# Half of the loads of x issued from ScalarE's DMA queue, the rest and the weights from SyncE's

## Chip, cores and metric

The kernel runs on one core of a Trainium2 chip. Its time is the device time of one execution in microseconds (us); less is better. One execution was also profiled: the profile gives each instruction's start and length on the engines PE (TensorE matmul), PEld (TensorE weight load), DVE (VectorE), ACT (ScalarE), POOL (GpSimd) and SP (SyncE), and what each of them waited for. SPq is the queue of SyncE's DMA issues.

## The reference

One layer of decayed linear attention with a gate, then a feed-forward part with routed low-rank adapters, each followed by a residual and a layer norm. x has 4 x 256 tokens of 512 features; there are 32 heads of 128.

```python
qkv = silu(x @ qkv_w.T)                       # 32 heads, q, k, v of 128
# per head, in blocks of 32 tokens:
scores = einsum(q, k) * diag_decay
out = scores @ v + (q * q_decay) @ kv
kv = kv * block_decay + (k * k_decay).T @ v
normed = norm_w * attn * rsqrt(mean(attn * attn) + eps)
x = layernorm(x + (sigmoid(x @ gate_w.T) * normed) @ out_w.T)
base = x @ base_W.T + base_b
w = softmax(x @ router_W.T + router_b)        # mapped to 8 experts
x = layernorm(x + base + 2 * ((x @ A.T) * w) @ B)
```

## The kernel before

Every product is made of float32 numbers split into a high and a low part (`xh`, `xl` for x; `wh`, `wl` or, for the first weights, `yh`, `yl`), with three matmuls for one: high by high, high by low, low by high. ACT makes the high parts, DVE the low ones. The heads go in 8 groups of 4. Weights come as blocks from `stream` through the two slots of `stage`; a block may only be loaded when the one two before it has been split (semaphore `t_lo`). All orders are written out by hand, one program for each engine, with semaphores between them, and all DMAs of this kernel stand in SyncE's program.

Only the start matters here. x arrives as eight pieces of 128 x 512 (`x_load(0)` to `x_load(7)`, from `xt` into `acc`, which is called `quad` in the code, 256 KB each), each with a semaphore of its own, `x_in[i]`. The first weight block arrives in three pieces: 128 KB (`w_first`), 128 KB (`w_in[0]`) and 256 KB (`w_in[1]`). ACT's `first_group` (from L738) takes them in a fixed order: first weights, x 0, second weights, x 1, third weights, x 2, then x 3 to x 7; before that it loads its activation table and runs a small warming SiLU (L1057). PE has seven matmuls on zeros (L2354) to begin with. Then `first_pieces(0)` to `first_pieces(7)` (L2190, L2196, L2199) do six matmuls for each piece of x: two of high by high, two with the weights' low part, two with x's low part. Piece 1 needs x 1 and the second weights, piece 2 needs x 2 and the third weights, pieces 3 to 7 only their x. The values of the first group (L2007 to L2009) and then all other work follow in PE's order.

After the loads of x, SyncE issues the second block of weights (L396, L397), two decay tables (L404), six small constants (L429) and the third block, which waits on `t_lo`.

Of the kernel before, what the change touches and what calls it, by code (L numbers as in the profile page):

```python
# [82 lines left out]
def load_no(g, name):  # L83

    if g == 0:
        return LOADS0.index(name)
    return len(LOADS0) + (g - 1) * len(LOADS) + LOADS.index(name)
# [22 lines left out]
def splits_of_load(m):  # L110

    if len(LOADS0) <= m < TAIL_LOAD and LOADS[(m - len(LOADS0)) % len(LOADS)] in ("va", "oa"):
        return 2 * m + 3
    return 2 * m + 2
# [36 lines left out]
def build(nc, stream, xt, x, decay, norm_w, base_b, lora_router, router_b, expert_map, ident_in, ones_in, fresh_in, out):  # L151
    ctx = ExitStack()
    with ctx:
# [3 lines left out]
        def sem(name):  # L157
            return ctx.enter_context(nc.semaphore(name))
# [81 lines left out]
        quad = acc[:, :, :].rearrange("p t n -> p (t n)").rearrange("p (q n) -> p q n", q=4)  # L240
# [9 lines left out]
        x_in = [sem(f"x_in{i}") for i in range(8)]  # L250
# [45 lines left out]
        def half(i):  # L296
            return slice(i * W, i * W + W)

        def tile(t):
            return slice(t * P, t * P + P)  # L300
# [80 lines left out]
        @block.sync  # L381
        def _(sp):
            def block_load(m):

                s = m % 2
                if m >= 2:
                    sp.wait_ge(t_lo, splits_of_load(m - 2))
                sp.dma_start(stage[:, s, 0, :], stream[m, :, 0, :]).then_inc(t_in[s], 16)
                sp.dma_start(stage[:, s, 3:8:2, :], stream[m, :, 1:4, :]).then_inc(t_in[s], 16)

            def rows_load(m, n=2):

                s = m % 2
                if m >= 2:
                    sp.wait_ge(t_lo, splits_of_load(m - 2))
                sp.dma_start(stage[:, s, 0:n, :], stream[m, :, 0:n, :]).then_inc(t_in[s], 16)  # L396
                sp.dma_start(stage[:, s, n:2 * n, :], stream[m, :, n:2 * n, :]).then_inc(t_in[s], 16)  # L397

            def load_decay(h):
                if h >= HEADS:  # L400
                    return
                if h >= 2:
                    sp.wait_ge(s_full, 2 * (h - 2) + 2)
                sp.dma_start(dec[:, h % 2, :], decay[h]).then_inc(dec_in[h % 2], 16)  # L404

            def next_group(g, name):
                if g + 1 < GROUPS:
                    block_load(load_no(g + 1, name))
                else:
                    rows_load(TAIL_LOAD + ["qk0", "va", "vb"].index(name))  # L410

            def x_load(i):
                sp.dma_start(quad[:, i // 2, half(i % 2)], xt[i // 2, :, half(i % 2)]).then_inc(x_in[i], 16)

            sp.dma_start(stage[:, 0, 0:2, tile(0)], stream[0, :, 0:2, tile(0)]).then_inc(w_first, 16)
            x_load(0)
            sp.dma_start(stage[:, 0, 0:2, tile(1)], stream[0, :, 0:2, tile(1)]).then_inc(w_in[0], 16)
            x_load(1)
            sp.dma_start(stage[:, 0, 2:4, :], stream[0, :, 2:4, :]).then_inc(w_in[1], 16)
            for i in range(2, 8):  # L420
                x_load(i)
            rows_load(1)
            load_decay(0)
            load_decay(1)
            for dst, src in ((nw[:, :], norm_w), (ident[:, :], ident_in), (ones[:, :], ones_in),
                             (rb[:, :], router_b.partition_broadcast(P)),
                             (emap[:, :], expert_map.partition_broadcast(P)),
                             (fresh[:, :], fresh_in.partition_broadcast(P))):
                sp.dma_start(dst, src).then_inc(const_in, 16)  # L429
            rows_load(2)  # L430
            for g in range(GROUPS):
                h = HG * g
                if g > 0:
                    block_load(load_no(g, "oa"))
                    block_load(load_no(g, "ob"))
                    load_decay(h + 1)
                block_load(load_no(g, "g01"))
                block_load(load_no(g, "qk1"))
                load_decay(h + 2)
                block_load(load_no(g, "g23"))  # L440
                block_load(load_no(g, "qk2"))
                block_load(load_no(g, "qk3"))
                next_group(g, "qk0")
                load_decay(h + 3)
                next_group(g, "va")
                next_group(g, "vb")
                load_decay(h + 4)

            sp.wait_ge(v_lo, HEADS)
            for t in range(TT):  # L450
                sp.dma_start(res[:, t, :], x[tile(t), :]).then_inc(res_in[t], 16)
            rows_load(TAIL_LOAD + 3)
            sp.wait_ge(s_lo, 2 * HEADS)
            sp.dma_start(ar, lora_router).then_inc(ar_in, 16)
            sp.wait_ge(sq_added, 2 * HEADS)
            sp.dma_start(bb, base_b.partition_broadcast(P)).then_inc(bias_in, 16)
            rows_load(TAIL_LOAD + 4, 1)
            for t in range(TT):
                if t < STATS:
                    sp.wait_ge(out_ready, t + 1)  # L460
                else:
                    sp.wait_ge(last_ready, t - STATS + 1)
                sp.dma_start(out[tile(t), :], res[:, t, :]).then_inc(stored[t], 16)
            for t in range(TT):
                sp.wait_ge(stored[t], 16)


        @block.scalar
        def _(act):
            def copy(dst, src, **kw):  # L470
                return nc.scalar.activation(dst, src, ACT.Copy, **kw)  # L471

            def sums_hi(g, name, part):

                m = load_no(g, name)
                act.wait_ge(t_sum, load_no(g, name) - 2)
                wait_free(act, g, name, part)
                u0, u1 = (0, 3) if part == "A" else (3, 7)
                runs = pieces(g, name, u0, u1)
                for i, (slot, before, n) in enumerate(runs):  # L480
                    ins = copy(wh[:, slot:slot + n, :], stage[:, m % 2, u0 + before:u0 + before + n, :])
                    if i == len(runs) - 1:
                        ins.then_inc(t_hi, 1)

            def rows_hi(m, slot, e, head=None):

                act.wait_ge(t_in[m % 2], 32 * ((m + 1) // 2))
                kw = {} if head is None else {"scale": nw[:, head:head + 1]}
                copy(wh[:, slot:slot + 2, :], stage[:, m % 2, 2 * e:2 * e + 2, :], **kw).then_inc(t_hi, 1)

            def u2_copy(n):
                act.wait_ge(p_done[1], n + 1)
                act.wait_ge(c12_added, n)
                if n == 0:
                    act.wait_ge(d_out, 10)
                elif place_of(n) == G01:
                    act.wait_ge(o_added, added_no(group_of(n), "c12", 0))
                copy(ps[:, B1, :], ps[:, B0, :]).then_inc(cp01, 1)
# [2133 lines left out]
```

## Time and profile before

| | |
|---|---|
| time, median of 3 runs | 996.95 us (996.23 to 997.51) |
| the profiled execution | 996.55 us, of which the span of instructions is 994.8 us |
| PE busy | 982.2 us, 99% of the span |
| DVE, ACT, POOL busy | 82%, 71%, 46% |
| DMA, mean over the span | 58 GB/s |
| DMA queues used by the kernel | one |

Times in the trace count from the first instruction. 1.75 us of the execution lie outside the span. A DMA's row on SPq is its issue; its landing is later, and shows as what an engine waited for.

### The profile page before, as it was taken

What the parts mean: (1) busy time and instruction counts of PE and PEld (TensorE: products, weight loads), DVE (VectorE), ACT (ScalarE), POOL (GpSimd) and SP (SyncE); (2) the same over time, 40 slices, a digit from 0 to 9 for tenths busy, and PEclk for the clock granted to TensorE, in tenths of its full rate; (3) what the DMA queues carried; (4) which work ended last, traced back from release to release, by engine and by line L of the source; (5) the groups of instructions that cost most, each with busy time, mean ns of one, the idle gap of its engine ahead of it and who ended that gap; (6) DMA issues with size and microseconds to landing.
All of it is one profiled execution on the core that took longest, in us unless ns stands there. A gap on an engine that the chain in (4) does not pass through costs nothing.

```text
span 994.8 us, 15911 instructions
## 1 busy us (share of the span) xinstructions
PE 982.2 (99%) x5569; PEld 860.6 (87%) x5569; DVE 815.9 (82%) x1122; ACT 710.0 (71%) x1197; POOL 456.0 (46%) x426
## 2 busy tenths in 40 slices
PE   8999999999999999999999999999999999999997
PEld 7878998889888898889988898888988899888896
DVE  6767887888967988779877889778887788899876
ACT  6677885788767785778857887677857788587653
POOL 1352564446453463534644464544635345531423
PEclk9999999999999999999999999999999999999999
DMA  6121111201121112212112111110122121110402
GB/s 211 30 64 46 64 48 48 71 30 52 51 65 51 35 47 72 63 44 66 45 55 66 30 52 51 64 51 30 51 72 64 38 73 38 56 52 22 159 12 85
DMA packets 52799, 57.78 MB, mean 58 GB/s; under 512 B 4336, under 2 KB 47728, under 8 KB 52720
## 3 DMA queue, kind: packets, MB, share of 16 engines
q1 hardware_dynamic: 52720, 56.77, 18.3%
q8 instruction: 45, 0.74, 0.3%
q14 instruction: 34, 0.28, 0.1%
HBM read 54.65 MB, written 2.10 MB: 57 GB/s over the span
## 4 chain that ended last, share of the span: by engine, by line
PE 93%; DMA 1%; ACT 1%; DVE 1%; issue 1%; POOL 1%; SPq 0%; POOLq 0%; ACTq 0%; DVEq 0%
PE ps L2013 25%; PE ps L2014 24%; PE ps L2015 24%; PE ps L2007 3%; PE ps L2009 3%; PE ps L2008 3%; PE ps L2110 2%; PE ps L2104 2%; PE ps L2106 2%; PE ps L2105 1%; PE ps L2124 1%; DMA stage<-stream 1%; PE ps L2108 1%; PE ps L2126 1%; DVE wl L1179 1%
## 5 line engine op out<-in xcount | busy, mean ns | idle before, releaser
L1884 POOL TENSOR_TENSOR stage<-stage 128x512 f32<-128x512 f32 x75 | 106.6, 1421 | 354.6 <-DMA stage<-stream 290.8
L2013 PE MATMUL ps<-xh,wh 128*128 128x512 f32 x658 | 260.0, 395 | 1.4 <-ACT stg L517 1.0
L2014 PE MATMUL ps<-xl,wh 128*128 128x512 f32 x658 | 257.0, 391 | 0.0
L2015 PE MATMUL ps<-xh,wl 128*128 128x512 f32 x658 | 256.2, 389 | 0.0
L1179 DVE TENSOR_TENSOR wl<-stage,wh 128x768 fp32r<-128x768 f32 (+3 forms) x183 | 201.3, 1117 | 28.4 <-ACT wh L471 27.7
L471 ACT ACTIVATE wh<-stage 128x768 fp32r<-128x768 f32 (+3 forms) x183 | 147.4, 833 | 17.8 <-POOL stage L1891 8.1
L2015 PEld LDWEIGHTS ps<-xh,wl 128*128 128x128 f32 x658 | 123.6, 188 | 26.8
L2013 PEld LDWEIGHTS ps<-xh,wh 128*128 128x128 f32 x658 | 123.7, 188 | 25.4 <-issue 1.8
L1927 POOL TENSOR_TENSOR sqacc<-sqacc,sq 128x512 f32<-128x512 f32 x64 | 92.8, 1451 | 110.9 <-ACT sq L629 110.9
L2014 PEld LDWEIGHTS ps<-xl,wh 128*128 128x128 f32 x658 | 123.7, 188 | 21.9
L471 ACT ACTIVATE ps<-ps 128x512 f32<-128x512 f32 x150 | 87.0, 584 | 65.0 <-PE ps L2015 65.0
L2013 PE MATMUL ps<-wh,xh 128*128 128x256 f32 (+1 forms) x423 | 122.8, 290 | 0.0
L2015 PE MATMUL ps<-wh,xl 128*128 128x256 f32 (+1 forms) x423 | 121.7, 288 | 0.0
L2014 PE MATMUL ps<-wl,xh 128*128 128x256 f32 (+1 forms) x423 | 121.5, 287 | 0.0
L1891 POOL TENSOR_TENSOR stage<-stage 128x256 f32<-128x256 f32 x75 | 81.0, 1080 | 5.9
L2013 PEld LDWEIGHTS ps<-wh,xh 128*128 128x128 f32 x423 | 80.8, 191 | 0.4
L2014 PEld LDWEIGHTS ps<-wl,xh 128*128 128x128 f32 x423 | 80.9, 191 | 0.3
L2015 PEld LDWEIGHTS ps<-wh,xl 128*128 128x128 f32 x423 | 80.8, 191 | 0.0
L1887 POOL TENSOR_TENSOR stage<-stage 128x256 f32<-128x256 f32 x75 | 68.4, 912 | 5.9
L1179 DVE TENSOR_TENSOR s<-ps,s 128x768 fp32r<-128x768 f32 x64 | 61.0, 953 | 10.1 <-ACT s L471 9.9
L471 ACT ACTIVATE s<-ps 128x768 fp32r<-128x768 f32 x64 | 51.7, 808 | 22.3 <-DVE ps L1259 22.2
L1253 DVE TENSOR_TENSOR ps<-ps,dec 128x768 f32<-128x768 f32 x64 | 61.1, 955 | 0.0
(224 smaller groups left out, 2320.9 us busy)
## 6 DMA issues: line engine op xcount, KB each, us to landing
stage<-stream SPq DMA_DIRECT2D x75, 384.0 KB, 3.4
stage<-stream SPq DMA_DIRECT2D x79, 128.0 KB, 2.1
dec<-decay SPq DMA_DIRECT2D x32, 192.0 KB, 2.4
stage<-stream SPq DMA_DIRECT2D x13, 256.0 KB, 3.1
acc<-xt SPq DMA_DIRECT2D x8, 256.0 KB, 6.0
v<-x SPq DMA_DIRECT2D x8, 256.0 KB, 5.8
out<-v SPq DMA_DIRECT2D x8, 256.0 KB, 2.0
y_home<-lora_router SPq DMA_DIRECT2D x1, 512.0 KB, 5.1
```

The costliest lines, as they stand in the source:

```text
L471: return nc.scalar.activation(dst, src, ACT.Copy, **kw)
L1179: return nc.vector.tensor_tensor(dst, full, f32(hi), ALU.subtract)
L1253: nc.vector.tensor_tensor(att_banks(e, 0, SC), att_banks(e, 0, SC), dec[:, h % 2, :].unsqueeze(1).broadcast_to([P, 2, SC]), ALU.mult)\
L1884: nc.gpsimd.tensor_tensor(stage[:, s, 1:5:3, :], stage[:, s, 0:6:5, :], stage[:, s, 7:8, :].broadcast_to([P, 2, U]), ALU.add).then_inc(t_p ...
L1887: nc.gpsimd.tensor_tensor(stage[:, s, 2, :], stage[:, s, 1, :], stage[:, s, 5, :], ALU.add)\
L1891: nc.gpsimd.tensor_tensor(stage[:, s, 6, :], stage[:, s, 2, :], stage[:, s, 3, :], ALU.add)\
L1927: nc.gpsimd.tensor_tensor(sqacc[:, e, :], sqacc[:, e, :], sq[:, :], ALU.add).then_inc(sq_added, 1)
L2007: nc.tensor.matmul(dst, wt[0], mv_[0], start=start, stop=False)
L2008: nc.tensor.matmul(dst, wt[0], mv_[1], start=False, stop=False)
L2013: nc.tensor.matmul(dst, wt[0], mv_[0], start=start, stop=False, skip_group_check=True)
L2014: nc.tensor.matmul(dst, wt[0], mv_[1], start=False, stop=False, skip_group_check=True)
L2015: return nc.tensor.matmul(dst, wt[1], mv_[0], start=False, stop=stop, skip_group_check=True)
```

## The change

`x_load` for pieces 0, 2, 4 and 6 moves from SyncE's program to the head of ScalarE's, ahead of the activation table. SyncE issues the three pieces of the first weights one behind another and then x 1, 3, 5, 7. Destinations, sizes and semaphores stay.

```diff
-            x_load(0)
             sp.dma_start(stage[:, 0, 0:2, tile(1)], stream[0, :, 0:2, tile(1)]).then_inc(w_in[0], 16)
-            x_load(1)
             sp.dma_start(stage[:, 0, 2:4, :], stream[0, :, 2:4, :]).then_inc(w_in[1], 16)
-            for i in range(2, 8):
+            for i in range(1, 8, 2):
                 x_load(i)
             rows_load(1)
             load_decay(0)
...
         @block.scalar
         def _(act):
+            def x_load(i):
+
+                act.dma_start(quad[:, i // 2, half(i % 2)], xt[i // 2, :, half(i % 2)]).then_inc(x_in[i], 16)
+
+            for i in range(0, 8, 2):
+                x_load(i)
+
```

SyncE's program from its start, before: `stage<-stream` are weights, `acc<-xt` pieces of x; the first `acc<-xt` is x 0, the second x 1, the six behind the last weights x 2 to x 7.

```order
1 L415 DMA stage<-stream 128x2x128
2 L413 DMA acc<-xt 128x512
3 L417 DMA stage<-stream 128x2x128
4 L413 DMA acc<-xt 128x512
5 L419 DMA stage<-stream 128x512
6 L413 DMA acc<-xt 128x512 x6
7 L396 DMA stage<-stream 128x512
8 L397 DMA stage<-stream 128x512
```

The same of the changed kernel: the four `acc<-xt` are now x 1, 3, 5 and 7.

```order
1 L415 DMA stage<-stream 128x2x128
2 L416 DMA stage<-stream 128x2x128
3 L417 DMA stage<-stream 128x512
4 L413 DMA acc<-xt 128x512 x4
5 L396 DMA stage<-stream 128x512
6 L397 DMA stage<-stream 128x512
```

x 1 stays the fourth issue of SyncE; the third weights, 256 KB, now stand ahead of it where x 0 stood, and four issues are gone from the queue.

ScalarE's program from its start, before:

```order
0 L468 UNCONDITIONAL_BRANCH
1 L1057 ACT_TABLE_LOAD
2 L1057 ACTIVATE warm<-half_power 128x8
3 L471 ACTIVATE yh<-stage 128x2x128
4 L471 ACTIVATE xh<-acc 128x512
5 L471 ACTIVATE yh<-stage 128x2x128
6 L471 ACTIVATE xh<-acc 128x512
```

And of the changed kernel:

```order
0 L466 UNCONDITIONAL_BRANCH
1 L470 DMA acc<-xt 128x512 x4
2 L1062 ACT_TABLE_LOAD
3 L1062 ACTIVATE warm<-half_power 128x8
4 L476 ACTIVATE yh<-stage 128x2x128
5 L476 ACTIVATE xh<-acc 128x512
6 L476 ACTIVATE yh<-stage 128x2x128
7 L476 ACTIVATE xh<-acc 128x512
```

Four issues stand ahead of the table load; the order behind it is the same.

## Rows read from the trace of the kernel before

**Rows 1.** The page: busy time and the chain that ended last, by line

```profile
PE 982.2 (99%) x5569; PEld 860.6 (87%) x5569; DVE 815.9 (82%) x1122; ACT 710.0 (71%) x1197; POOL 456.0 (46%) x426
PE 93%; DMA 1%; ACT 1%; DVE 1%; issue 1%; POOL 1%; SPq 0%; POOLq 0%; ACTq 0%; DVEq 0%
```

**Rows 2.** The chain in order of time, 0 to 10 us: start, us, what

```profile
2.19 4.72 DMA acc<-xt
6.93 0.64 ACT xh L471
7.62 0.74 PE ps L2190 x2
```

**Rows 3.** Waits of PE from 10 us to the end: us, times, longest

```profile
PE ps L2104 <- issue: 2.0, 4, 0.8
PE ps L2013 <- ACT stg L517: 1.0, 2, 0.6
```

**Rows 4.** Timeline of PE: start, us, engine, line, operation, idle before

```profile
1.44 3.22 PE L2354 MATMUL ps<-s 128*128 128x512 f32 x7 [1.44 <-DVE s L1648]
5.32 0.73 PE L2190 MATMUL ps<-xh,yh 128*128 128x512 f32 x2 [0.66 <-ACT xh L471]
...
6.35 0.62 PE L2199 MATMUL ps<-xl,yh 128*128 128x512 f32 x2
7.62 0.74 PE L2190 MATMUL ps<-xh,yh 128*128 128x512 f32 x2 [0.64 <-ACT xh L471]
...
9.13 0.62 PE L2190 MATMUL ps<-xh,yh 128*128 128x512 f32 x2
9.59 0.62 PE L2196 MATMUL ps<-xh,yl 128*128 128x512 f32 x2
```

**Rows 5.** Timeline of ACT, 0 to 14 us

```profile
0.72 1.28 ACT L1057 ACT_TABLE_LOAD   x1 [0.72 <-PEq L2625]
2.01 0.21 ACT L1057 ACTIVATE warm<-half_power 128x8 f32<-128x8 f32 x1
3.52 0.42 ACT L471 ACTIVATE yh<-stage 128x256 fp32r<-128x256 f32 x1 [1.31 <-DMA stage<-stream]
4.64 0.63 ACT L471 ACTIVATE xh<-acc 128x512 fp32r<-128x512 f32 x1 [0.70 <-DMA acc<-xt]
...
9.55 0.63 ACT L471 ACTIVATE xh<-acc 128x512 fp32r<-128x512 f32 x1 [0.67 <-DMA acc<-xt]
```

**Rows 6.** Busy times by stretch; the last three columns are PEclk, DMA share, GB/s

```profile
2.00:3.00 1.00, 1.00 (x4) 0.77 (x3) 0.00 (x0) 0.21 (x1) 0.00 (x0) 1.00 0.78 257
6.00:7.00 1.00, 0.97 (x5) 0.46 (x3) 0.32 (x1) 0.07 (x1) 0.00 (x0) 1.00 0.56 213
7.00:8.00 1.00, 0.38 (x2) 0.34 (x3) 0.40 (x1) 0.96 (x2) 0.00 (x0) 1.00 0.69 205
8.00:9.00 1.00, 1.00 (x6) 0.78 (x5) 1.00 (x3) 0.87 (x2) 0.00 (x0) 1.00 0.96 344
1.00:9.00 8.00, 6.26 (x19) 4.32 (x20) 3.24 (x7) 4.46 (x8) 0.71 (x1) 1.00 0.73 229
9.00:13.00 4.00, 4.00 (x19) 3.31 (x18) 3.38 (x6) 3.17 (x5) 0.00 (x0) 1.00 1.04 394
```

**Rows 7.** The tile acc: its issues on SPq (duration ns min/median/max), and landings

```profile
L413 SPq DMA_DIRECT2D acc<-xt x8: 432/442/527, 1.2 to 5.6; - x8
DMA to landing us min/median/max: 3.4/6.0/6.6
```

**Rows 8.** Timeline of SP, 0 to 12 us

```profile
2.19 0.47 SPq L413 DMA_DIRECT2D acc<-xt  x1
```

**Rows 9.** The end: PE's last matmul, and the granted clock after it

```profile
988.24 0.39 PE L2015 MATMUL ps<-vh,q 128*128 128x512 f32 x1
990.00:992.00 2.00, 0.00 (x0) 0.00 (x0) 1.50 (x5) 0.00 (x0) 1.27 (x3) 0.71 0.57 208
992.00:995.00 3.00, 0.00 (x0) 0.00 (x0) 0.20 (x1) 0.00 (x0) 0.00 (x0) 0.50 0.57 214
```

## The prediction, made before the changed kernel was run

> **What bounds the kernel now.** I read the page first. PE is busy for 982.2 of 994.8 us and is 93% of the chain that ended last [rows 1], so time can only be won or lost where PE stands still. Next I read PE's waits from 10 us to the end: the two largest entries are 2.0 and 1.0 us in total [rows 3], and none names a load of x. Behind the first pieces, then, PE's work is one rigid train, and whatever delays its start delays the end by as much.
>
> Where the train begins is told by the chain of the first 10 us. It runs through a load of x that was issued at 2.19 and took 4.72 us to land, at 6.91, then 0.64 us of ACT, then the first matmuls of piece 1 at 7.62 [rows 2]. The timeline of PE shows the same from its side: piece 0 starts at 5.32, its last pair at 6.35, and PE stands still before piece 1; pieces 1 and 2 then follow without a gap [rows 4]. So the quantity that decides is the landing of x 1, not that of x 0. ACT waits once more, 0.67 us for x 3, which it takes at 9.55 [rows 5], but that wait costs PE nothing: piece 3 starts where piece 2 ends.
>
> **What the change removes.** If x 1 were there in time, piece 1 could follow piece 0. A pair of matmuls passes in 0.46 us (9.13 to 9.59 [rows 4]), so piece 0's last pair is through at 6.35 + 0.46 = 6.81, and 7.62 - 6.81 = 0.81 us is all that an earlier x 1 can give. An earlier x 0 gives nothing by itself. SyncE loses four issues, about 4 x 0.44 = 1.8 us of its queue [rows 7]. What stood behind them comes that much earlier, but PE waits for none of it [rows 3]: nothing.
>
> **What it adds on ACT.** Four issues stand ahead of the table load. The trace has no issue from ACT; the nearest rows are SyncE's, 0.44 us each [rows 7]. So 0.72 + 4 x 0.44 = 2.48, the table load to 3.76, the warming SiLU to 3.97, the first weights to 4.39 [rows 5]. ACT would turn to x 0 at about 4.4, and it did so at 4.64 before. The cover is thus the 1.31 and 0.70 us that ACT idled for DMAs in rows 5, and it is nearly used up. As upper bound I let an issue take twice as long, if two queues hinder each other: 1.76 us more, x 0 begun at 6.15 and done at 6.78, piece 0 on PE from 6.8 to 8.3 (it takes 1.5 us from its start to the end of its last pair), and piece 1 0.7 us later than now. Below: nothing. I take nothing, because the term below is larger and covers it (the two run side by side).
>
> **What it does to x 1.** SyncE issues x 1 as its fourth DMA, as before, at about 2.19 [rows 8]. Before, 768 KB were asked for up to and with it: weights 128, x 0 256, weights 128, x 1 256. In the changed kernel SyncE's own queue holds 128 + 128 + 256 + 256, again 768 KB, but ScalarE's queue asks for 1,024 KB of x 0, 2, 4, 6 in the same two microseconds. If the DMA engines serve the two queues by turns, byte for byte, 768 KB of the other queue pass before x 1 is through: it stands at 1,536 KB. That is exactly where x 3 stood before (512 KB of weights and four pieces of x). x 3 was taken at 9.55 by an ACT that had waited for it [rows 5]. Putting x 1 there moves the decisive step from 6.93 to 9.55: **+2.6 us**.
>
> The DMA engines are the scarce thing here, which is why order matters: between 1 and 9 us they moved 229 GB/s, between 9 and 13 us 394 GB/s [rows 6]. Moving x in two queues adds no bytes and takes none away; it only lets x 2, x 4 and x 6, not needed before x 1 is split, run ahead of x 1. The Trainium skill (DMA: Bandwidth & Descriptors, section Issuing engines are not separate DMA queues) says that DMAs issued from different engines run on the same 16 DMA engines and interleave, so that a second issuer saves issue time only. By that rule the change wins nothing on transfers, and the sum would be the one above; this trace has one queue and can't show it.
>
> Bounds of this term. Below: between 6 and 8 us the DMA engines were busy only 0.56 and 0.69 of the time and moved 213 and 205 GB/s, though all eight pieces had been issued by 6.1 [rows 6, 7]. If a second queue fills those holes and the rate is 394 GB/s from 3 us on, when 0.28 MB had passed (the 257 of rows 6 and a trickle ahead of it), the 1.57 MB are through at 3 + 1.29 / 0.394 = 6.3. x 3 landed 1.3 us after as many bytes had passed (229 GB/s x 8 us = 1.83 MB by 9.0, less 0.8 us at 344 GB/s, gives 1.57 MB at 8.2; ACT took it at 9.55 [rows 5, 6]). So x 1 would land at 7.6, +0.7. Above: if the queues take turns by descriptor and not by bytes, the first two weight loads (512 B pieces) are outrun by all 1,024 KB of ScalarE's queue, and x 1 stands at 1,792 KB, 0.26 MB or 0.7 us later (at 0.34 to 0.39 MB per us) [rows 6]: +3.3. I take +2.6, since it has a row of its own, x 3's, and the price needs no new rate.
>
> Downstream nothing gives it back: ACT takes third weights, x 2 and x 3 behind x 1 in 0.63 us steps as now, piece 2 and the rest stay on PE's heels, and x 3, at 2,048 KB in the new order, would be reached 1.3 us after 1,536 KB (0.52 MB at 394 GB/s), about 10.9, before ACT wants it at 9.55 + 3 x 0.66 = 11.5.
>
> **Sum.** Removed 0, ACT's issues 0 (covered), x 1 later +2.6: on the profiled execution 996.55 + 2.6 = 999.15. The median of the runs is 0.4 us above that execution, so measured as the median is, 996.95 + 2.6 = **999.5 us**. A difference of about 0.2%, 2.0 us, is what a measurement of this kernel tells from no change, so this forecast lies just outside it.
>
> **The rivals.**
> *The clock falls in the new gap.* PE would stand still from 6.8 to about 10.2, 3.4 us. Before, gaps of 0.66 and 0.64 us left the granted clock at 1.00 (2.4 GHz) [rows 4, 6]. At the end of the kernel PE's last matmul stops at 988.63, and the mean clock of 0.71 between 990 and 992 means that it fell from 1.00 to 0.50 (1.2 GHz) at 992 - 2 x 0.58 = 990.8, after 2.2 us without a matmul [rows 9]. So the new gap is long enough for it by this trace. Price: the seven matmuls at the kernel's start took 0.46 us each [rows 4], the pace of the lower level (the column of the granted clock, 1.00 there, doesn't show it), against 0.23 later; as many again would cost 7 x 0.23 = 1.6 us, 1001.1 in all. Against it: the pieces on either side of the gap are dense. The Trainium skill (TensorE: Matmul & The Clock Gate, section Part 1) says that an idle PE returns to the lower clock; it would decide for this rival if the gap were as long as I expect.
>
> *The second queue feeds the DMA engines better.* The holes at 6 to 8 us speak for it; then x 1 lands between 7.6 and 8.9, the cost is 0.7 to 1.9 us, the middle 998.3: not told from no change.
>
> *No loss, or a small gain.* This is the side opposite to my forecast. The mechanism: ScalarE's queue doesn't get half of the DMA engines but serves behind SyncE's, or its first bytes start late, so that x 1 has only the 512 KB of its own queue ahead of it and lands by 6.9 or before. It decides if x 1 lands before 7. It is worth at most the 0.81 us above: 996.1 to 997. A gain above 0.2% is not possible at this place, as only 0.81 us are there.
>
> *ACT late by its own issues* gives +0.7 at most, 997.6, as worked out; it is hidden wherever x 1 is later.
>
> **How the numbers follow.** x 1 in x 3's place at full clock 0.33 (own range 998.8 to 1000.3); the same with the clock fallen 0.18 (1000.3 to 1001.6); better fed, ACT's delay with it, 0.37 (997.5 to 998.9); no loss or a gain 0.09 (996.1 to 997.2); anything else 0.03. Slower by over 0.2% holds most of the first, the second and the last: 0.53. Same: 0.45. Faster: 0.02, for the drift between measurements. The range leaves out the fourth case, and the upper part of the second: 997.3 to 1001.1.
>
> **What would show it.** In the profile after, the ACT row of the second `xh<-acc` should start near 9.5 with DMA acc<-xt as its releaser and an idle time near 4 us; PE's gap ahead of the second L2190 near 3.4 us; ACT's table load near 2.5, and its first `yh` near 4.0. If the clock fell, a stretch after the gap shows 0.50 and matmuls of 0.46 us. From piece 1 on all rows should be those of before shifted by the same amount. The forecast is wrong if x 1 is taken before 8.9, or if ACT's issues take so long that x 0 is the later one.

## The result, and the profile after

The changed kernel takes 999.84 us, median of 15 runs (997.44 to 1001.95); the kernel before, run beside it 15 times, 996.89 us. The ratio is 1.0026, 95% interval 1.0017 to 1.0035: about 0.26% or 2.6 us slower by the ratio, 2.95 us by the medians. The profiled execution took 998.60 us with a span of 996.8, that is 2.05 us more than the profiled one of before.

The chain of the changed kernel from the third issue of SyncE on, in order of time (start, us, what); it answers to [rows 2]:

```profile
1.74 0.46 SPq L417
2.20 0.04 issue
2.25 6.91 DMA acc<-xt
9.15 0.02 issue
9.18 0.64 ACT xh L476
9.81 0.04 issue
9.86 0.72 PE ps L2195 x2
```

x 1 is issued 0.06 us later than before and lands 2.25 us later. The timeline of ACT shows the same from its side, and answers to [rows 5]:

```profile
0.72 1.91 ACTq L470 DMA_DIRECT2D acc<-xt  x4
2.66 1.28 ACT L1062 ACT_TABLE_LOAD   x1 [2.66 <-issue]
3.96 0.21 ACT L1062 ACTIVATE warm<-half_power 128x8 f32<-128x8 f32 x1
4.79 0.42 ACT L476 ACTIVATE yh<-stage 128x256 fp32r<-128x256 f32 x1 [0.63 <-DMA stage<-stream]
5.12 0.61 ACT L476 ACTIVATE xh<-acc 128x512 fp32r<-128x512 f32 x1
5.84 0.42 ACT L476 ACTIVATE yh<-stage 128x256 fp32r<-128x256 f32 x1
9.18 0.63 ACT L476 ACTIVATE xh<-acc 128x512 fp32r<-128x512 f32 x1 [2.92 <-DMA acc<-xt]
```

The four issues are done at 2.63 and the table load follows at once. The first weights come later than before (4.79 against 3.52), although they are still SyncE's first issue, and x 0 is begun 0.48 us later. Neither matters beside the 2.92 us for which ACT waits for x 1.

The timeline of PE answers to [rows 4]:

```profile
1.44 3.36 PE L2359 MATMUL ps<-s 128*128 128x512 f32 x7 [1.44 <-DVE s L1653]
5.78 1.22 PE L2195 MATMUL ps<-xh,yh 128*128 128x512 f32 x2 [0.99 <-ACT xh L476]
6.80 1.05 PE L2201 MATMUL ps<-xh,yl 128*128 128x512 f32 x2
7.65 1.05 PE L2204 MATMUL ps<-xl,yh 128*128 128x512 f32 x2
9.86 0.72 PE L2195 MATMUL ps<-xh,yh 128*128 128x512 f32 x2 [1.15 <-ACT xh L476]
10.42 0.63 PE L2201 MATMUL ps<-xh,yl 128*128 128x512 f32 x2
```

Piece 1 starts at 9.86 instead of 7.62: 2.24 us, of which 2.0 are left at the end of the span. Piece 0 holds a surprise. Its pairs follow each other in 0.85 us (6.80 to 7.65), where before they took 0.46: the lower of the two levels of the clock (1.2 GHz). The column of the granted clock shows 1.00 here, as it did during the warming matmuls, so the level is read from the pace; the one-queue run below has the same pace where the column shows 0.50. From piece 1 on the pace is the full one (2.4 GHz). In this execution the clock rose between 8.50 and 9.86 us, while PE stood still, and cost nothing at the end: piece 1 waited for x 1 in any case.

How the two queues shared the DMA engines is shown by the queues' totals (packets, MB, share of 16 engines) from 0 to 5 us; q10 is ScalarE's, q1 SyncE's:

```profile
q10 hardware_dynamic: 306, 0.56, 42.6%
q1 hardware_dynamic: 510, 0.26, 17.7%
```

ScalarE's queue moved twice the bytes of SyncE's while SyncE's held the weights and x 1. From 5 to 9.15 us, when x 1 landed, the shares turned:

```profile
q1 hardware_dynamic: 568, 0.99, 64.4%
q10 hardware_dynamic: 270, 0.49, 36.4%
```

Together 2.3 MB had passed by then, against 1.83 MB by 9.0 before. The DMA engines were better fed, as one rival had it, between 1 and 9 us at 280 GB/s against 229 [rows 6]:

```profile
1.00:9.00 8.00, 6.28 (x13) 3.97 (x13) 1.84 (x4) 2.85 (x5) 0.71 (x1) 1.00 0.88 280
```

Still x 1 came late, since more had been put ahead of it. How much more is shown by the totals from 0 to 7.9 us:

```profile
q10 hardware_dynamic: 562, 1.03, 45.5%
q1 hardware_dynamic: 828, 0.79, 29.5%
```

The weights and x 1 are 768 KB, 0.79 MB, of SyncE's queue. When that much of it had passed, so had nearly all of ScalarE's 1,024 KB (1.05 MB): 1.82 MB together, about 1,780 KB if SyncE's queue is served in order. That is not the 1,536 KB of turns byte for byte but nearly the 1,792 KB of the prediction's upper bound. x 1 landed 1.3 us later, at 9.15.

### The profile page after: what moved, and what is told of

Same layout as the page of the kernel before. It is cut to its first block, busy times and chain, and to the rows that moved or that the text cites. A ratio compares the mean times of both kernels' runs of the same rounds, so it can differ in the third digit from the quotient of the medians.

```text
span 996.8 us, 15911 instructions
## 1 busy us (share of the span) xinstructions
PE 983.4 (99%) x5569; PEld 861.5 (86%) x5569; DVE 814.8 (82%) x1122; ACT 708.7 (71%) x1197; POOL 456.1 (46%) x426
## 3 DMA queue, kind: packets, MB, share of 16 engines
q10 hardware_dynamic: 576, 1.05, 0.4%
## 4 chain that ended last, share of the span: by engine, by line
PE 93%; DMA 2%; DVE 1%; ACT 1%; issue 1%; POOL 1%; SPq 0%; POOLq 0%; ACTq 0%; DVEq 0%
PE ps L2018 24%; PE ps L2019 24%; PE ps L2020 24%; PE ps L2012 3%; PE ps L2014 3%; PE ps L2013 3%; PE ps L2115 2%; PE ps L2109 2%; PE ps L2111 2%; PE ps L2110 1%; PE ps L2129 1%; DMA stage<-stream 1%; PE ps L2113 1%; PE ps L2131 1%; DMA acc<-xt 1%
## 5 line engine op out<-in xcount | busy, mean ns | idle before, releaser
L1184 DVE TENSOR_TENSOR s<-ps,s 128x768 fp32r<-128x768 f32 x64 | 61.0, 954 | 10.4 <-ACT s L476 10.1
```

The lines of the kernel that those rows point to most:

```text
L1184: return nc.vector.tensor_tensor(dst, full, f32(hi), ALU.subtract)
```

## The experiments

Each was compared with the kernel before on the same chip; the times are medians. "KB to x 1" counts both queues as if they took turns byte for byte (by its trace the changed kernel had about 1,780 there); "x 1" is the start of the second `xh<-acc` on ACT in the one profiled execution.

| kernel | KB to x 1 | x 1, us | ratio (95%) |
|---|---|---|---|
| before | 768 | 6.93 | 1 |
| changed | 1,536 | 9.18 | 1.0026 (1.0017 to 1.0035) |
| changed, again | 1,536 | 8.97 | 1.003 (1.002 to 1.004) |
| one queue, x 1 seventh | 1,536 | 9.77 | 1.0025 (1.0014 to 1.0036) |
| x 4, x 6 from ACT | 1,280 | 7.60 | 1.0014 (1.0005 to 1.0023) |
| x 4 from ACT | 1,024 | 7.41 | 1.0006 (0.9998 to 1.0015) |
| x 4 from ACT, small pieces | 1,024 | 7.05 | 1.0003 (0.9995 to 1.0012) |
| x 0 from ACT | 768 | 6.37 | 0.9997 (0.9986 to 1.0008) |
| x 0, x 1 from ACT | 1,024 | 5.79 | 1.0002 (0.9992 to 1.0012) |
| four small constants from ACT | 814 | 8.56 | 1.0033 (1.002 to 1.0046) |
| four tiny loads from ACT | 769 | 6.69 | 1.0001 (0.9992 to 1.001) |
| changed, 12 warming matmuls | 1,536 | 8.70 | 1.0032 (1.002 to 1.0044) |
| before, 9 warming matmuls | 768 | 6.54 | 0.9995 (0.9986 to 1.0004) |
| x 0, x 1 from ACT, 9 warming | 1,024 | 5.59 | 0.9991 (0.9981 to 1.0001) |

**The changed kernel again.** No edit.

> The changed kernel unaltered, to see how its times spread and where the clock rises in another execution. If the delay is x 1's landing alone, ACT takes x 1 near 9.2 again, and the time is 2.0 to 2.6 us above the kernel before. If a clock that rises late in some executions adds to it, the runs spread over more than 2 us, some 3 us or more above the kernel before, and a profile of such a one would show matmuls of 0.43 to 0.46 us each behind piece 1.

998.96 us (996.78 to 1002.07, 12 runs) against 996.25. x 1 was taken earlier than in the first profile, at 8.97, and yet the profiled execution was slower, 999.88 us. PE's timeline says why:

```profile
9.65 1.22 PE L2195 MATMUL ps<-xh,yh 128*128 128x512 f32 x2 [1.15 <-ACT xh L476]
10.67 1.05 PE L2201 MATMUL ps<-xh,yl 128*128 128x512 f32 x2
11.52 1.05 PE L2204 MATMUL ps<-xl,yh 128*128 128x512 f32 x2
12.38 1.05 PE L2195 MATMUL ps<-xh,yh 128*128 128x512 f32 x2
13.23 0.83 PE L2201 MATMUL ps<-xh,yl 128*128 128x512 f32 x2
```

Here the slow pace (0.85 us for a pair) lasts through pieces 1 and 2 and ends near 13.6. The first value matmul shows the loss. It is the first row of L2012 on PE, in the first profile and in this one:

```profile
19.51 0.39 PE L2012 MATMUL ps<-wh,xh 128*128 128x512 f32 x1
```

```profile
21.16 0.39 PE L2012 MATMUL ps<-wh,xh 128*128 128x512 f32 x1
```

1.65 us later, of the same kernel with x 1 earlier by 0.21: 1.86 us come from the slow pace behind piece 1. The spans differ by 1.3 (998.1 and 996.8).

**One queue with the same order.** All on SyncE:

```diff
             x_load(0)
             sp.dma_start(stage[:, 0, 0:2, tile(1)], ...).then_inc(w_in[0], 16)
-            x_load(1)
+            x_load(2)
             sp.dma_start(stage[:, 0, 2:4, :], ...).then_inc(w_in[1], 16)
-            for i in range(2, 8):
+            for i in (4, 1, 6, 3, 5, 7):
```

> One queue again, all on SyncE, but with x 1 at the place in the bytes that the two queues give it: first weights, x 0, second weights, x 2, third weights, x 4, x 1, x 6, x 3, x 5, x 7. Theory (it is the 1,536 KB up to and with x 1 that set its landing): ACT takes x 1 at 9.2 to 9.6, time +2 to +3 us over the kernel before, without any second queue. Rival (two queues as such, or ACT's issues ahead of its table load, cost the time): x 1 lands near 7 to 7.5, time within 0.7 us of the kernel before.

998.91 us against 996.25, x 1 at 9.77, a little above the forecast. x 1 alone, put seventh among the pieces and weights, makes a slow-down as large as the changed kernel's, with no second queue and nothing on ACT. That the ratios agree to 0.0001 is partly chance: here x 1 stands at 1,536 KB and the DMA engines moved 216 GB/s between 1 and 9 us, in the changed kernel at about 1,780 KB and they moved 280. ACT's row, then two rows of PE, and then the busy times in three stretches with the granted clock as the third column from the right:

```profile
9.77 0.63 ACT L471 ACTIVATE xh<-acc 128x512 fp32r<-128x512 f32 x1 [3.73 <-DMA acc<-xt]
...
12.02 1.05 PE L2190 MATMUL ps<-xh,yh 128*128 128x512 f32 x2
12.88 1.05 PE L2196 MATMUL ps<-xh,yl 128*128 128x512 f32 x2
...
10.00:12.00 2.00, 1.55 (x6) 1.24 (x7) 1.57 (x3) 1.94 (x4) 0.00 (x0) 0.97 1.05 394
12.00:15.00 3.00, 3.00 (x8) 2.31 (x7) 3.00 (x6) 3.00 (x7) 0.00 (x0) 0.50 1.02 308
15.00:18.00 3.00, 3.00 (x14) 2.50 (x13) 2.08 (x4) 2.08 (x5) 0.00 (x0) 0.95 0.44 160
```

This is the clock rival in the open. PE had run piece 0 at the full level, stood still for 3.74 us, took up piece 1 at 10.45, and the clock then fell to 0.50 (1.2 GHz) through 12 to 15 us, about 1.5 us after PE had taken up work again. A pair takes 0.86 us there (12.02 to 12.88), the slow pace of the rows above. From piece 1 to the first value matmul it took 11.3 us instead of the 9.69 of before: the fall cost 1.6 us in this execution.

**How many bytes ahead.** Three kernels keep SyncE's order of before and let ACT issue loads that no one needs early; the third lays x 4 out so that the same 256 KB pass in pieces of 512 bytes.

```diff
+            for i in (4, 6):
+                x_load(i)
```

> SyncE keeps the order of before up to x 2 and x 3; ACT issues only x 4 and x 6, 512 KB that no one needs early, so x 1 stands at 1,280 KB. Theory of bytes: half the price, x 1 taken by ACT at 8.2 to 8.9, time +1.2 to +2.0 us. If instead the SyncE order of the changed kernel (third weights ahead of x 1) were the cause, x 1 lands at 7.0 and the time is that of before within 0.4 us.

997.71 us against 995.92, x 1 at 7.60: below the forecast for the landing, inside that for the time. This profiled execution, 995.39 us, is the fastest of its twelve, and x 1 later by 0.67 us does not explain the 1.8 us of the medians; the rest is open. Third weights stand behind x 1 here, so the later place of x 1 doesn't need them ahead of it.

```diff
+            act.dma_start(quad[:, 2, half(0)], xt[2, :, half(0)]).then_inc(x_in[4], 16)
```

> SyncE keeps the order of before; ACT issues x 4 alone, 256 KB in 128 pieces of 2 KB. Counting bytes, x 1 stands at 1,024 KB and is taken at 7.3 to 7.9; counting pieces, 128 more than before, about the same. Time +0.3 to +1.0 us over the kernel before.

```diff
+            act.dma_start(quad[:, 2, half(0)].rearrange("p (c n) -> p c n", c=4),
+                          x4.rearrange("c p n -> p c n")).then_inc(x_in[4], 16)
```

> The same 256 KB of x 4 from ACT, but out of an array in which they lie so that they pass in 512 pieces of 512 bytes. If bytes set the landing of x 1, it is taken as in the run with x 4 whole, within 0.3 us, and the times agree. If the pieces of the other queue that pass between its own do, x 1 is taken 0.7 us or more later, toward 8.6 as with the small constants in 512 pieces, and the time is 1 to 2 us higher than with x 4 whole.

997.02 and 996.94 us against 996.53, x 1 at 7.41 and 7.05. Four times as many pieces made nothing later, so the number of pieces has no price of its own here. It doesn't tell which turns the queues take: in both runs all 256 KB of x 4 (0.26 MB on ScalarE's queue) had passed by 5 us, and turns by byte and turns by piece both put them ahead of x 1. Along 768, 1,024, 1,280 and 1,536 KB of the table the take of x 1 goes 6.37 to 6.93, 7.05 to 7.41, 7.60, 8.70 to 9.77: more bytes ahead, later x 1, on single profiles each, as long as x 1 itself is on SyncE's queue. Neighbouring steps are not told apart: the same DMA program gave 6.93 and 6.54 (before, with 7 and 9 warming matmuls), and 9.18, 8.97 and 8.70 (changed).

**Only x 0 from ACT.** SyncE then issues first weights, second weights, x 1, third weights, x 2 to x 7.

> Only x 0 is issued from ACT; SyncE issues first weights, second weights, x 1, third weights, x 2 to x 7. x 1 has 768 KB up to and with it, over both queues, as in the kernel before. Theory of bytes: x 1 lands at 6.5 to 7.0, time 0 to 0.5 us below the kernel before. Rival that a second queue or the issues on ACT cost: +0.7 us or more.

996.33 us against 996.25. A second queue by itself costs nothing that this measurement tells, and x 1 came 0.56 us earlier, yet the median shows no gain. Its profiled execution, 993.37 us, must not be read as one: the first value matmul starts at 17.00 against 17.31 before, 0.3 us, while the spans are 991.6 and 994.8. The other 2.9 us arose behind it, where the programs are alike; PE's waits after 20 us add up to 3.5 us before and 1.8 in this execution, and the rest has no row that explains it.

**x 0 and x 1 from ACT.** SyncE issues the first weights and x 2 to x 7.

```diff
-            for i in range(0, 8, 2):
+            for i in (0, 1):
                 x_load(i)
```

> ACT issues x 0 and x 1 only; SyncE issues the three pieces of the first weights and then x 2 to x 7. x 1 is the second load of its queue: 512 KB of its own queue and as many of the other pass up to its end, 1,024 KB. Theory of bytes: x 1 taken by ACT at 7.3 to 8.0, time +0.4 to +1.0 us over the kernel before. If a load on ACT's queue is served ahead of SyncE's, x 1 lands before 6.9 and the time falls by up to 0.8 us.

995.90 us against 995.92. My count of bytes fails for the landing: ACT took x 1 at 5.79 without waiting.

```profile
4.96 0.61 ACT L476 ACTIVATE xh<-acc 128x512 fp32r<-128x512 f32 x1
5.48 0.40 ACT L476 ACTIVATE yh<-stage 128x256 fp32r<-128x256 f32 x1
5.79 0.61 ACT L476 ACTIVATE xh<-acc 128x512 fp32r<-128x512 f32 x1
```

The queues' totals from 0 to 5 us show that nearly all of ACT's two loads had passed, and less of SyncE's:

```profile
q10 hardware_dynamic: 286, 0.52, 34.6%
q1 hardware_dynamic: 602, 0.38, 23.9%
```

So the turns are not byte for byte; ScalarE's queue, with the 2 KB pieces against SyncE's 512-byte ones, had the larger part in the first microseconds, as in the changed kernel. And the earliest x 1 but one of the series brought no time. In the profiled execution piece 0 and piece 1 ran at the pace of 0.85 us for a pair, to 10.91; but at 998.35 us this is the slowest of the twelve, so it doesn't speak for the median.

**ACT's issues without the bytes.** Four small constants move from SyncE to the head of ACT's program; then four loads of 256 bytes each in their place.

```diff
+            for dst, src in ((ones[:, :], ones_in),
+                             (rb[:, :], router_b.partition_broadcast(P)),
+                             (emap[:, :], expert_map.partition_broadcast(P)),
+                             (fresh[:, :], fresh_in.partition_broadcast(P))):
+                act.dma_start(dst, src).then_inc(const_in, 16)
```

> All loads of x as before on SyncE, but four small constants (46 KB together) issued from ACT ahead of its table load, so that ACT's path has the four issues without the bytes. Theory that ACT's issues are covered: the table load starts near 2.6 as in the changed kernel, ACT takes x 0 at 5.1 to 5.3 and x 1 near 7.0; time within 0.4 us of the kernel before. Rival that ACT's late start costs: x 1 is split no earlier than 7.6, +0.7 us or more.

999.23 us against 996.25: the rival's side. ACT's own path was not late, x 0 was taken at 4.62, but x 1 only at 8.56:

```profile
4.62 0.63 ACT L474 ACTIVATE xh<-acc 128x512 fp32r<-128x512 f32 x1
5.24 0.42 ACT L474 ACTIVATE yh<-stage 128x256 fp32r<-128x256 f32 x1
8.56 0.63 ACT L474 ACTIVATE xh<-acc 128x512 fp32r<-128x512 f32 x1 [2.90 <-DMA acc<-xt]
...
1.00:9.00 8.00, 6.28 (x13) 3.97 (x13) 1.83 (x4) 3.28 (x6) 0.71 (x1) 1.00 0.70 193
```

```diff
+            for i in range(4):
+                act.dma_start(ones[32 * i:32 * i + 32, :], ones_in[32 * i:32 * i + 32, :]).then_inc(const_in, 16)
```

> Like the run with small constants from ACT, but the four issues are quarters of the smallest constant: 1 KB and 128 pieces of 8 bytes in all, against 46 KB and 512 pieces there. ACT's path has the same four issues. If what delays x 1 is the number of DMAs that two queues take turns with, x 1 is taken by ACT at 8.2 to 8.9 again and the time is 2 to 3 us over the kernel before. If it is the number of pieces (or bytes) that pass ahead of x 1, it is taken at 6.9 to 7.3 and the time is within 0.7 us of the kernel before.

996.15 us against 995.83, x 1 at 6.69. The issues are therefore innocent: the same four, with the table load at 2.69, cost nothing that shows. With the small constants the DMA engines as a whole moved less (193 GB/s between 1 and 9 us against 229 before). Of the 3.3 us by which the first value matmul came later (20.62 against 17.31), x 1 gives 1.6; the other 1.7 are the slow pace of PE, to about 12.9 us. Three of the four constants spread one short row of HBM over all 128 partitions, and the tiny loads do not; but they are also 512 pieces of 8 to 240 bytes against 128 of 8 bytes. The run with x 4 in 512 pieces of 512 bytes excludes the number of pieces as such. Whether the common source or many pieces this small are the cause was not tried.

**More warming matmuls.**

```diff
-WARMUP = 7
+WARMUP = 12
```

> The changed kernel with twelve matmuls on zeros instead of seven at PE's start; at 0.46 us each they end near 7.0, so that PE's gap ahead of piece 1 has matmuls in more of it (piece 0 then runs from 7.0 to about 8.4, still ahead of x 1). If a late or fallen clock makes the slower executions of the changed kernel, this one's runs lie closer together, +2.0 to +2.4 us over the kernel before. If x 1's landing alone makes the spread, its runs are as wide as those of the changed kernel and the median is the same.

998.73 us against 995.92 (997.95 to 1000.2, 6 runs). The spread is narrower than the changed kernel's, but the ratio is not lower. On six runs this settles little. With nine, in the kernel before and in that with x 0 and x 1 from ACT:

> The kernel before with nine matmuls on zeros instead of seven, so that at the lower clock they reach to 5.6, where piece 0 starts, and close the first gap. If executions of the kernel before lose time to a clock that rises late after that gap, the median falls by 0.3 to 1 us and the runs lie closer together. If not, it is 0 to 0.3 us slower.

> x 0 and x 1 from ACT as in the run of that name, whose PE had no gap behind piece 0, and nine matmuls on zeros, so that PE has no gap from 1.4 us on. [...] Expected 1 to 2 us below the kernel before. If the clock is not the cause of the spread, the time is that of the run with seven, within 0.3 us of the kernel before.

995.48 and 995.22 us against 995.83. The second had no gap on PE and piece 0 at 5.35, and its ratio of 0.9991 has an interval that just reaches 1 (1.0001). It is the best of the series, and not shown to be faster than the kernel before; the forecast of 1 to 2 us was missed, with 0.6 by the medians.

## Why the prediction was nearly right

*What bounds the kernel.* Right in this pair: 2.24 us at piece 1 became 2.0 at the end. But the train behind the start is less rigid than the prediction has it. From the first value matmul to the end it took 974.6 to 977.5 us in the fourteen profiled executions, whether the start was early or late.

*Removed: nothing.* Right. The kernels that took x 1 earlier by 0.56 and 1.14 us showed no gain in their medians, and the earliest first value matmul of all profiles (16.35, with x 0 and x 1 from ACT and nine warming matmuls) is only 0.96 us ahead of the kernel before, against a forecast prize of 0.81.

*ACT's issues, taken as covered.* Right, by the run with the tiny loads; the four issues took 1.91 us, against 1.76. The forecast of 4.4 for x 0 was 0.7 early, because the first weights landed later, not because of ACT.

*x 1 in x 3's place, +2.6 us.* The mechanism was right: bytes that the second queue lets pass delay x 1, and one queue with x 1 that far back is as slow (1.0025, two queues 1.0026). The size was a little high. ACT took x 1 at 9.18, 8.97 and, with 12 warming matmuls, 8.70: +2.25, +2.04 and +1.8. That it came so near is luck, since two errors met in it. The turns between the queues were not byte for byte: x 1 stood at about 1,780 KB, not 1,536. And the DMA engines moved 280 GB/s, not 229. With the first error alone the prediction's own working gives +3.3; with the second alone, about +1.6, an estimate from the changed trace, in which 1,536 KB had passed by 7.2 us and landings followed 1.3 us later.

*The clock.* Here the step failed in part. I let it stay up through the gap or fall, and gave the fall 0.18. The gap of 3.4 us, from which the fall was argued, did not come about: PE's last idle time ahead of piece 1 was 1.15 us, as piece 0 began 0.46 us later and ran at the slow pace. The trace of one execution does not show that it can also rise late: piece 0 was slow in both profiles of the changed kernel, and in one the slow pace lasted to 13.6 us and cost 1.86. The median of 2.95 us above before is more than x 1's landing gives, and a late clock, seen to cost time in one of the two profiles, could be the rest. That it makes up that rest in the median is argued, not shown: the run with twelve warming matmuls, whose profile has the full pace from piece 0 on, did not lower it. So the median forecast of 999.5 against 999.84 is nearer than its working deserves.

The Trainium skill (DMA: Bandwidth & Descriptors, Issuing engines are not separate DMA queues) says that such DMAs interleave on the same engines; the two rows of q1 and q10 agree. The same section of the Trainium skill says that only issue time is saved; here the rate rose as well, 280 against 229 GB/s, and the measurement decides. In the profiles with 512 KB or more on ScalarE's queue it was 276 to 290, in those of the kernel before, the same with nine warming matmuls and the one-queue order 216 to 237. The Trainium skill (TensorE: Matmul & The Clock Gate, Part 1) has an idle PE fall back to the lower clock; the stretch at 0.50 behind a gap of 3.74 us agrees, though it began only when PE had worked again for about 1.5 us.

## What to carry to other kernels

A second DMA queue doesn't by itself make a load early; it takes away the order in which loads land. Put on it what is needed first (x 1 as ScalarE's second load was taken at 5.79 instead of 6.93), or nothing that can overtake what PE waits for: here nearly all of ScalarE's 1,024 KB, 768 of them not needed yet, passed ahead of the one piece that decided. Count for the deciding transfer all bytes that any queue may pass before it, not only an equal share. The transfer that had that place in the old trace gives an estimate without a new rate, but it carries the old queue's rate with it.

## What the runs showed of the hardware

- The moment at which the clock rises is not fixed. Of one kernel, two executions had the full pace from 9.86 and from about 13.6 us on, although their first matmuls both began at 1.44. Of the fourteen profiled executions nine had it at piece 0 and five had not: besides these two the small constants (full pace from about 12.9), x 0 and x 1 from ACT (10.9) and x 4 whole (10.1). The idle time ahead of piece 0 doesn't separate them: 0.51 to 0.99 us in the five, 0 to 1.32 in the nine. Why some rise late stays open.
- A gap on PE can cost more than its length: behind 3.74 us without a matmul the one-queue run lost another 1.6 us at 0.50.
- Behind the first value matmul the same program took 977.5 us (before, 994.8 - 17.31) and 974.6 us (x 0 from ACT, 991.6 - 17.00) in single executions. One profiled time can't tell effects below 3 us. Its early rows can, down to the 0.4 to 0.5 us by which the same load landed apart in different executions.
- Four loads of 46 KB together, issued on a second queue at the start, delayed a load on the first by 1.6 us and the kernel by 0.33% (part of it the clock, in its profile), more than 256 KB of x did (0.06%, not told from none).
